# Attention on one Trainium2 core: the softmax division moved from the probabilities to the outputs of a chunk of 512 queries

## The reference

```python
xs = ln_c(x).reshape(N, C, S).transpose(0, 2, 1)        # C = 512, S = 1024
q = xs @ Wq.T + bq;  k = xs @ Wk.T + bk;  v = xs @ Wv.T + bv
# 8 heads of 64
energy = einsum('nhqd,nhkd->nhqk', q, k)
attn = softmax(energy / sqrt(64), axis=3)
out = einsum('nhql,nhld->nhqd', attn, v)
out = out.reshape(N, -1, C) @ Wo.T + bo                 # heads are not moved back beside each other
x = x + out
t = tokens(x);  t = t + ffn(ln_t(t))                    # a three-layer table of nibble arithmetic on a few channels
```

## Time and profile before

| what | value |
|---|---|
| three runs | 2573.52, 2580.71, 2581.93 us |
| median | 2580.71 us |
| the profiled execution | 2580.17 us, its span 2578.4 us |
| PE busy | 2480.2 us, 96% |
| DVE, ACT, POOL busy | 75%, 67%, 35% |
| mean granted clock of PE | 0.991 |
| share of the DMA engines | 27.5% |

### The profile page before, as it was taken

One profiled execution on the slowest core, in us unless ns is written; L12 is line 12 of the kernel. 1 busy time (PEld: TensorE's weight loads), 2 busy tenths in 40 slices (PEclk: granted clock), 3 DMA queues, 4 the chain that ended last, 5 costly groups with the idle time before them and its releaser, 6 DMA issues.

```text
span 2578.4 us, 37154 instructions
## 1 busy us (share of the span) xinstructions
PE 2480.2 (96%) x13216; PEld 2030.9 (79%) x13216; DVE 1928.8 (75%) x3607; ACT 1735.9 (67%) x3083; POOL 893.4 (35%) x804
## 2 busy tenths in 40 slices
PE   7999999999999999999999999999999999999986
PEld 6788878888788787887878878788777887778874
DVE  5777777787777877778677786777867777677766
ACT  4777557775677746777477774777747776477744
POOL 1344414443144432444313433244422444134431
PEclk9999999999999999999999999999999999999997
DMA  7223203341133312224123331232403223033210
GB/s 265 72 70 110 97 28 91 86 131 66 50 82 76 121 66 66 73 72 135 50 68 76 78 130 43 78 85 60 155 17 92 73 70 143 23 93 78 72 64 33
DMA packets 80357, 215.13 MB, mean 83 GB/s; under 512 B 10256, under 2 KB 10416, under 8 KB 74416
## 3 DMA queue, kind: packets, MB, share of 16 engines
q1 hardware_dynamic: 80176, 212.77, 27.5%
HBM read 102.63 MB, written 25.17 MB: 50 GB/s over the span
## 4 chain that ended last, share of the span: by engine, by line
PE 85%; DVE 7%; ACT 4%; issue 1%; POOL 1%; DMA 0%; SPq 0%; ACTq 0%; DVEq 0%
PE pT L462 16%; PE pJ L428 10%; PE pO L477 9%; PE pO L478 9%; PE pS L449 8%; PE pS L450 8%; PE po L612 7%; PE pv L585 7%; PE pv L428 3%; DVE PL L876 2%; DVE nmax L844 1%; PE pt L570 1%; POOL PR L383 1%; ACT PR L692 1%; PE ph L517 1%
## 5 line engine op out<-in xcount | busy, mean ns | idle before, releaser
L383 POOL TENSOR_SCALAR PR<-PR,rinv 128x1024 f32<-128x1024 f32 x512 | 578.5, 1130 | 1240.0 <-DVE rinv L848 1240.0
L726 ACT ACTIVATE PH<-pT 128x512 fp32r<-128x512 f32 x1024 | 557.5, 597 | 361.3 <-PE pT L462 347.7
L876 DVE TENSOR_TENSOR PL<-pT,PH 128x512 fp32r<-128x512 f32 x1024 | 657.4, 684 | 178.1 <-ACT PH L726 176.0
L844 DVE TENSOR_REDUCE nmax<-pS 128x1 f32<-128x1024 f32 x512 | 623.8, 1218 | 150.5 <-PE pS L450 149.5
L692 ACT ACTIVATE PR<-pS,nmax 128x1024 f32<-128x1024 f32 x512 | 574.8, 1123 | 4.7 <-DVE nmax L844 1.5
L462 PEld LDWEIGHTS pT<-ident,PR 128*128 128x128 f32 x4096 | 466.9, 141 | 129.1 <-POOL PR L383 46.0
L462 PE MATMUL pT<-ident,PR 128*128 128x128 f32 x4096 | 545.4, 275 | 22.4 <-DVE PL L876 15.2
L477 PE MATMUL pO<-PH,VS 128*128 128x512 f32 x1024 | 418.1, 408 | 6.3 <-DVE PL L876 6.3
L449 PE MATMUL pS<-KHL,QS 128*128 128x512 f32 x1024 | 411.9, 402 | 5.8 <-DMA KHL<-KHL 3.6
L478 PE MATMUL pO<-PL,VS 128*128 128x512 f32 x1024 | 404.0, 395 | 0.0
L450 PE MATMUL pS<-KHL,QS 128*128 128x512 f32 x1024 | 402.9, 393 | 0.0
(11 more groups left out here) (171 smaller groups left out, 3048.9 us busy)
## 6 DMA issues: line engine op xcount, KB each, us to landing
KHL<-HL SPq DMA_DIRECT2D x192, 256.0 KB, 3.6
X<-in_x SPq DMA_DIRECT2D x64, 512.0 KB, 6.2
WQ<-wqk_split SPq DMA_DIRECT2D x62, 512.0 KB, 4.3
QS<-HL SPq DMA_DIRECT2D x192, 128.0 KB, 3.1
WO<-wo_split SPq DMA_DIRECT2D x16, 1024.0 KB, 6.8
out<-X SPq DMA_DIRECT2D x16, 1024.0 KB, 4.5
KHL<-wv_split SPq DMA_DIRECT2D x14, 1024.0 KB, 8.5
KHL<-KHL SPq DMA_DIRECT2D x16, 512.0 KB, 4.2
```

The source lines that it names most:

```text
L383: pool.tensor_scalar(PR[g % 2][:, :], PR[g % 2][:, :], M["rinv"][:, g:g + 1], 1.0, ALU.mult, ALU.mult)\
L726: act.activation(PH[ck % 2][:, 4 * half:4 * half + 4, (g % 4) * P:(g % 4 + 1) * P], pT[half][:, :].rearrange("p (k n) -> p k n", k=4), ACT ...
L844: dve.tensor_reduce(nmax[:, g:g + 1], pS[g % 2][:, :], AX.X, ALU.max, negate=True).then_inc(S["a_max"], 1)
L876: dve.tensor_tensor(PL[ck % 2][:, ks, qs], pT[half][:, :].rearrange("p (k n) -> p k n", k=4), f32(PH[ck % 2][:, ks, qs]), ALU.subtract).th ...
```

## The change

PR is no longer multiplied: `turn` waits for the exponential alone (a_exp). DVE takes a chunk's four columns of reciprocals in one instruction, 128 a run in place of 512. SP writes them to a row of 512 numbers in memory (`reciprocals_out`, 512 pieces of four bytes) and reads this row back into 64 partitions of RB (`reciprocals_in`), 128 times each. POOL then multiplies the 64×512 outputs in OT by RB and adds b_v (`scale_output`), once per chunk; OB is a plain copy on ACT. The bank pO and OB are now set free by the new semaphore a_osum, which DVE raises after OT = pO + OB; a_o is raised by POOL after both of its operations, and H waits for it. One more small load brings b_v to the lower partitions.

The tables changed with it. The 60 steps between edges are now written into them, in the same order except on POOL, whose row names only the steps that do something. At an edge PE now has T5 to T7 ahead of O0 and O1, V2 and V3 two pieces of B later, P1 ahead of L23 and Y0, and R spread as R0 to R3, R4 R5, R6 R7 between the steps A; ACT has H0 and H1 ahead of the T's and H3 behind N0. The setup pieces W and D3 of START stand at other places, as do F3, H3 and O7's neighbours in LAST.

```diff
-    "a_w0": 48, "a_w1": 48, "a_scores": 64, "a_max": 64, "a_exp": 64, "a_recip": 64, "a_norm": 64, "a_tr": 128,
+    "a_w0": 48, "a_w1": 48, "a_scores": 64, "a_max": 64, "a_exp": 64, "a_recip": 16, "a_row": 256, "a_rows0": 128, "a_rows1": 128, "a_osum": 16, "a_omul": 16, "a_tr": 128,
...
+        rs_s = nc.dram_tensor("rinv_rows", (2 * HEADS, 512), F32, kind="Internal").ap()
...
-    "vector": """H0 H1 E67 T0 H2 T1 T2 T3 T4 T5 O0 T6 T7 O1 H3 O2 N0 O3 O4 O5 O6 O7 B0 U0 U1 B1 B2 U2 U3 V0 U4 U5 U6 U7
+        E57 E58 E59 E60 E61 E62 E63 H0 H1 T0 H2 T1 T2 T3 T4 T5 T6 T7 E67 O0 O1 O2 N0 O3 O4 H3 O5 O6 O7 B0 B1 U0
...
-    "gpsimd": """H0 N0 F0 A0 A1 A2 A3""",
+    "gpsimd": """E7 E8 E11 E12 E15 E16 E19 E20 E23 E24 E27 E28 E31 E32 E35 E36 E39 E40 E43 E44 E47 E48 E51 E52 E56 E60
+        E64 H0 E68 N0 F0""",
...
+    def reciprocals_out(i, ck):
+        wait("a_recip", i, ck + 1)
+        sp.dma_start(dram["rs"][ck].rearrange("(j p) -> p j", p=P), M["rinv"][:, 4 * ck:4 * ck + 4],
+                     allow_slow_non_contiguous=True).then_inc(S["a_row"], 16)
+
+    def reciprocals_in(i, ck):
+        wait("a_row", i, 16 * (ck + 1))
+        if ck >= 2:
+            wait("a_omul", i, ck - 1)
+        elif i > 0:
+            wait("a_omul", i - 1, 2 * HEADS)
+        half = slice(ck % 2 * D, (ck % 2 + 1) * D)
+        sp.dma_start(M["RB"][half, :], dram["rs"][ck].unsqueeze(0).to_broadcast([D, 512])).then_inc(S[f"a_rows{ck % 2}"], 16)
 
...
+        reciprocals_out(i, 0)
...
+                reciprocals_in(i, k)
+                reciprocals_out(i, k + 1)
...
+        reciprocals_in(i, 12)
+        for k in range(2):
+            if i + 1 < N_IMG:
                 wait("a_scores", i, ST * (HEADS - 1 + k))
                 sp.dma_start(f32(WV[k].rearrange("p k n -> p (k n)")), dram["wv"][:, k, :]).then_inc(S["f_wv"], 16)
+            if k == 1:
+                reciprocals_in(i, 13)
+            reciprocals_out(i, 13 + k)
+        reciprocals_in(i, 14)
+        reciprocals_out(i, 15)
         wait("a_pv", i, 2 * HEADS)
         for t in range(CT):
             sp.dma_start(M["X1"][:, t, :], dram["x"][i, :, t, :]).then_inc(S[f"b_x{t}"], 16)
+        reciprocals_in(i, 15)
         if i + 1 < N_IMG:
...
+    def scale_output(img, ck):
+        h, n = divmod(ck, 2)
+        part = slice(n * D, (n + 1) * D)
+        o = M["OT"][part, :, h * P:(h + 1) * P]
+        wait("a_osum", img, ck + 1)
+        wait("a_proj_lo", img, min(ck + 1, PER["a_proj_lo"]))
+        if ck == 2 * HEADS - 1:
+            wait("b_bias", img, 2 * CT)
+        wait(f"a_rows{n}", img, 16 * (h + 1))
+        pool.tensor_tensor(o, o, M["RB"][part, :].rearrange("d (j m) -> d j m", j=CT), ALU.mult).then_inc(S["a_omul"], 1)
+        wait("a_omul", img, ck + 1)
+        pool.tensor_scalar(o, o, M["b_v"][part, h:h + 1], None, ALU.add).then_inc(S["a_o"], 1)
+        wait("a_o", img, ck + 1)
+
     for kind, img, g in order:
...
-        if kind == "A" and 0 <= g < STEPS:
-            wait("a_recip", img, g + 1)
-            pool.tensor_scalar(PR[g % 2][:, :], PR[g % 2][:, :], M["rinv"][:, g:g + 1], 1.0, ALU.mult, ALU.mult)\
-                .then_inc(S["a_norm"], 1)
+        if kind == "A" and 0 <= g < STEPS + 5:
+            if g >= 8 and g % 4 == 0:
+                scale_output(img, g // 4 - 2)
...
-        wait("a_norm", i, g + 1)
+        wait("a_exp", i, g + 1)
...
-                wait("a_o", i, ck)
+                wait("a_osum", i, ck)
...
-                wait("a_o", i, ck - 1)
-            act.activation(OB[ck % 2][:, :], pO[D:P, :], ACT.Identity,
-                           bias=b_v[D:P, ck // 2:ck // 2 + 1]).then_inc(S["a_obot"], 1)
+                wait("a_osum", i, ck - 1)
+            act.activation(OB[ck % 2][:, :], pO[D:P, :], ACT.Copy).then_inc(S["a_obot"], 1)
...
-    def recip(i, g):
-        wait("a_exp", i, g + 1)
-        dve.reciprocal(rinv[:, g:g + 1], rsum[:, g:g + 1]).then_inc(S["a_recip"], 1)
+    def recip(i, ck):
+        wait("a_exp", i, 4 * ck + 4)
+        dve.reciprocal(rinv[:, 4 * ck:4 * ck + 4], rsum[:, 4 * ck:4 * ck + 4]).then_inc(S["a_recip"], 1)
 
     def attend(i, g):
         if g < 0:
             rowmax(i, 0)
             rowmax(i, 1)
-            recip(i, 0)
...
+        if g + 1 < STEPS and g % 4 == 2:
+            recip(i, g // 4)
...
-                              OB[ck % 2][:, :].rearrange("d (j m) -> d j m", j=CT), ALU.add).then_inc(S["a_o"], 1)
```

More of the change, by code:

```diff
@@ L211 @@
-    "gpsimd": """N0 A0 A1 A2 A3""",
+    "vector": """T0 T1 T2 T3 T4 T5 T6 T7 N0 W0 B0 B1 B2 V0 W2 V1 B3 B4 B5 V2 W1 V3 W3 B6 B7 V4 V5 W4 W5 V6 V7 Q0 Q1 Q2
+        A-1 D3 A0 A1 A2 A3""",
+    "gpsimd": """N0""",
 }
 EDGE = {
-    "tensor": """T0 T1 E65 E66 E67 T2 T3 T4 O0 T5 T6 T7 O1 O2 O3 O4 O5 O6 O7 U0 U1 B0 B1 B2 U2 U3 V0 U4 B3 U5 B4 U6 U7 V1
-        V2 V3 B5 B6 B7 V4 V5 V6 F0 F1 V7 F2 F3 L0 Q0 L1 L10 L2 L11 L20 L3 L12 L21 Q1 Q2 L22 L13 P0 L23 P1 Y0 Q3
-        A0 R0 R1 R2 R3 R4 A1 R5 R6 A2 R7 A3""",
@@ L223 @@
-    "gpsimd": """H0 N0 F0 A0 A1 A2 A3""",
+    "tensor": """E4 E5 E6 E7 E8 E9 E10 E11 E12 E13 E14 E15 E16 E17 E18 E19 E20 E21 E22 E23 E24 E25 E26 E27 E28 E29 E30
+        E31 E32 E33 E34 E35 E36 E37 E38 E39 E40 E41 E42 E43 E44 E45 E46 E47 E48 E49 E50 E51 E52 E53 E54 E55 E56
+        E57 E58 E59 E60 E61 E62 E63 T0 T1 E65 E66 E67 T2 T3 T4 T5 T6 T7 O0 O1 O2 O3 O4 O5 O6 O7 U0 U1 B0 B1 B2
+        U2 U3 V0 U4 U5 B3 B4 U6 U7 V1 V2 B5 B6 V3 B7 V4 V5 V6 F0 F1 V7 F2 F3 L0 Q0 L1 L10 L2 L11 L3 L20 Q1 L12
+        L21 Q2 L22 L13 P0 P1 L23 Y0 Q3 A0 R0 R1 R2 R3 A1 R4 R5 A2 R6 R7 A3""",
@@ new lines @@
+    "scalar": """E4 E5 E6 E7 E8 E9 E10 E11 E12 E13 E14 E15 E16 E17 E18 E19 E20 E21 E22 E23 E24 E25 E26 E27 E28 E29 E30
+        E31 E32 E33 E34 E35 E36 E37 E38 E39 E40 E41 E42 E43 E44 E45 E46 E47 E48 E49 E50 E51 E52 E53 E54 E55 E56
+        E57 E58 E59 E60 E61 E62 E63 H0 H1 T0 T1 T2 T3 T4 H2 E67 T5 T6 T7 N0 H3 U0 U1 B0 B1 B2 U2 U3 V0 U4 U5 U6
+        U7 S0 B3 B4 V1 V2 B5 B6 V3 B7 V4 V5 F0 F1 V6 V7 F2 F3 L0 L1 L10 Q0 L2 L11 L20 L3 Q1 L12 L21 Q2 L22 L13
+        L23 A-1 Q3 A0 R0 R1 R2 R3 A1 R4 R5 A2 R6 R7 A3""",
@@ L230 @@
-    "vector": """E67 H0 H1 H2 O0 H3 O1 O2 O3 O4 O5 O6 U0 U1 U2 U3 S10 O7 S15 S11 U4 S12 U5 U6 U7 S13 S20 S25 S21 L0 S22
-        S23 L10 L1 L11 L2 L3 L12 S14 L13 S24""",
-    "gpsimd": """H0 F0 F2""",
+    "tensor": """E4 E5 E6 E7 E8 E9 E10 E11 E12 E13 E14 E15 E16 E17 E18 E19 E20 E21 E22 E23 E24 E25 E26 E27 E28 E29 E30
+        E31 E32 E33 E34 E35 E36 E37 E38 E39 E40 E41 E42 E43 E44 E45 E46 E47 E48 E49 E50 E51 E52 E53 E54 E55 E56
+        E57 E58 E59 E60 E61 E62 E63 E65 E66 E67 O0 O1 O2 O3 O4 O5 O6 U0 U1 U2 U3 O7 U4 U5 U6 U7 F0 F1 L0 L10 F2
+        L1 F3 L20 L11 L2 L21 L3 L12 Y10 L22 L13 R0 R1 R2 L23 R3 Y20 R4 R5 R6 R7""",
@@ new lines @@
+    "scalar": """E4 E5 E6 E7 E8 E9 E10 E11 E12 E13 E14 E15 E16 E17 E18 E19 E20 E21 E22 E23 E24 E25 E26 E27 E28 E29 E30
+        E31 E32 E33 E34 E35 E36 E37 E38 E39 E40 E41 E42 E43 E44 E45 E46 E47 E48 E49 E50 E51 E52 E53 E54 E55 E56
+        E57 E58 E59 E60 E61 E62 E63 E67 H0 H1 H2 H3 U0 U1 U2 U3 S10 U4 U5 U6 U7 S20 F0 F1 L0 L10 L1 F2 L20 F3
+        L11 L2 L3 L21 L12 L22 L13 R0 R1 R2 L23 R3 R4 R5 R6 R7""",
+    "vector": """E4 E5 E6 E7 E8 E9 E10 E11 E12 E13 E14 E15 E16 E17 E18 E19 E20 E21 E22 E23 E24 E25 E26 E27 E28 E29 E30
+        E31 E32 E33 E34 E35 E36 E37 E38 E39 E40 E41 E42 E43 E44 E45 E46 E47 E48 E49 E50 E51 E52 E53 E54 E55 E56
+        E57 E58 E59 E60 E61 E62 E63 E67 H0 H1 H2 O0 O1 O2 O3 O4 H3 O5 O6 U0 U1 U2 U3 S10 O7 S15 S11 U4 U5 U6 S12
+        U7 S13 S20 S25 S21 L0 S22 S23 L10 L1 L11 L2 L3 L12 S14 L13 S24""",
@@ L233 @@
+    "gpsimd": """E7 E8 E11 E12 E15 E16 E19 E20 E23 E24 E27 E28 E31 E32 E35 E36 E39 E40 E43 E44 E47 E48 E51 E52 E56 E60
+        E64 H0 E68 F0 F2""",
 }
@@ L242, in schedule @@
     for i in range(N_IMG):
-        order += [("A", i, g) for g in range(4, 64)] + work(EDGE if i + 1 < N_IMG else LAST, i)
+        order += [("A", i, g) for g in range(4, 4)] + work(EDGE if i + 1 < N_IMG else LAST, i)
     return order
@@ L616, in tensor_program @@
                 wait("b_res", i, 7 if n < ST // 2 else 8)
-                wait(*(("a_proj_out", i, 12), ("a_o", i, 16))[n])
+                wait(*(("a_proj_out", i, 12), ("a_osum", i, 16))[n])
             else:
@@ L674, in scalar_program @@
         "XT", "XH", "OH", "OT", "VS", "QS", "KHL", "PR", "PH", "OB", "X1", "HL", "QK", "WV"))
-    b_qk, b_v, nmax, rsum = (M[k] for k in ("b_qk", "b_v", "nmax", "rsum"))
+    b_qk, nmax, rsum = (M[k] for k in ("b_qk", "nmax", "rsum"))
     pS, pT, pt, pa, ph, pv = ([B[f"{n}{k}"] for k in range(c)] for n, c in (
```

36 lines of the change are left out of this document (14 added, 22 removed).

## The result

| kernel | median of the runs | ratio to the kernel before |
|---|---|---|
| before | 2577.9 us | |
| changed | 2686.8 us (2677.6 to 2687.9) | 1.0414, 95% interval 1.0398 to 1.0429 |

The account below looks back on a forecast made before the run. PE was taken as the bound, busy 2480.2 of 2578.4 us. From 2580.2 us, loop −8, image 0 −2 and edges −3.3 gave 2567 us; the 8-in-10 range was 2550 to 2592.

Parts of the forecast that it names:

- the two small transfers per chunk: SP's row write and read per chunk: 3.6 us landing each, 7.2 us together, hidden in 13.4 us, costing nothing.
- The rival of the late row: At the edge, late rows delay bo's additions and O6: 2591 us at 8.5 us a landing; 15% chance.
- the signs of being wrong: Closing list: loop windows not shortening, PE waiting for OL, landing above 6.7 us, or PE's products at another pace.
- The loop: Steps 4 to 63 of each image: OB earlier 0.5 us, shorter PL waits 0.5 us; 8 us saved in all.
- The waits for PL: PE's three waits per image for PL on DVE, 15.2 us in 24, to shorten to near 12 us.
- the window of 201.00 us: Steps 4 to 63 of an image: PE busy 198.31 us, 2.69 idle, so at most 21.5 us to gain.
- Image 0: Start of the first image: two transposition waits for POOL's product, 1.12 and 0.80 us, go; −2 us.
- The edges: Seven edges between images: 1.05 − 0.32 − 0.45 − 0.75 = −0.47 us each, −3.3 in all.
- The turnover: PE's O0 to O7 at an edge: PE idles 1.8 us before O2, O7 ends 1.05 us later.
- The results' chain: At each edge, DVE's results that R waits for begin 1.15 us earlier without sum wait and reciprocal; taken as −0.75 us.
- The copy of K: At each edge, P1 ahead of L23 and Y0 starts K's copy earlier, removing `scores(0)`'s 0.45 us wait.
- The tail: End of the last image, where H3 has more room: taken with the start as 0, ends ±2 us.

Follow-up runs that it names:

- the kernel with 16-byte pieces: Changed kernel with each row stored in partition order, 128 pieces of 16 bytes instead of 512 of 4, POOL reading RB strided: 2570.1 us, ratio 0.9967.
- the first of the two turnover kernels: Against the kernel with 16-byte pieces: last row read before X1's loads, chunk 15 scaled before bo's additions, turnover tables near their old order: 2563.5 us, ratio 0.9943.

## Why the prediction was wrong

The step that failed is one term: the two small transfers per chunk, priced at a landing of 3.6 us and a cost of nothing. The 3.6 us was that of copies of 256 KB, and the write has 2 KB in 512 pieces of four bytes. The read did land near it (3.9 us). The write took 10.4 and 18.4 us where it was read off the chain, and it costs 122 us, 104 of them through the transfers behind it. With this write taken out the kernel takes 2565.2 us, for a forecast of 2567. That it is so near is in part luck, as the last items below say.

- *The bounds.* The longest landing considered was 12.1 us, the landing of a small load. A load of whole rows says nothing on 512 touching pieces; the range was too narrow because no row resembled the operation and I bounded it all the same. The write was also taken as a latency for whoever waits for it. That is the larger part of the error: 104 us are paid without anyone waiting.
- *The rival of the late row* had 15% and named the right place: X1's loads, the additions of bo, PE at O. Its price of 24.5 us was for 8.5 us a landing; at 12.1 it gave 75, left out of the range, and the edges lost 81. It put PE's wait at O6 for H3; it is at O0's evacuation, since the additions themselves are late (57.4 us of DVE's waits were for them). It had no loop in it: I had written that with a late row only POOL would wait. POOL's queue also holds HL.
- *The Trainium skill*, DMA: Bandwidth & Descriptors, says in "Rules for kernel authors" that a strided last dimension becomes one descriptor per element, and in "Specifications" that pieces under 512 bytes are read, changed and written back. I named it as speaking against the 3.6 us and gave it no price. The runs agree only in part: 512 pieces of four bytes are dear side by side, but 64 bytes apart they land in 3.3 us.
- *The clock.* That PE's own products might follow each other at another pace stood among the signs of being wrong, and no step counted it. It is some 31 of the 122 us.
- *The loop*, −8 us: in the kernel with 16-byte pieces −8.6 (the eight loops sum to 1573.4 us for 1582.0). It is right in size and wrong in its split: OB, priced at 0.5 us an image, gave 0.94. The waits for PL, which were to shorten to 12 us in 24, are 18.2 us in 36. Of the 6.3 us for POOL's product 3.6 lay at step 57 of the images, not at the starts. And the window of 201.00 us is longer than the steps it stood for: within 197.6 us PE is not busy for 2.2, so that the whole of it is 18 us and not 21.5.
- *Image 0*, −2: 10.3 to 8.8 us from step 0 to 4, −1.5, but not by the waits. The time in which PE is not busy there is 2.1 and 2.0 us; its busy time fell from 8.20 to 6.79, since the half-clock stretch that the kernel before has there is absent.
- *The edges*, −0.5 each: +1.3 from the last exponential to the first, −1.5 on average in steps 0 to 4, together −0.2. The turnover was foreseen as +1.05 with PE waiting 1.8 us ahead of O2; it is +1.2 (the last O starts 36.06 us behind the last exponential, for 34.91) with a wait of 1.54. The results' chain gave more than −0.75. The copy of K gave −0.33 (PE's wait is left in one image of eight). The 0.32 us in V3 went, but a later value product waits 0.28 us for XL.
- *The tail*, 0: it was −3.0 us in that profile, 102.7 to 99.7. PE's waits there are the same; its busy time fell from 75.2 to 72.2. In all kernels whose last steps are the same, the tail goes from 98.5 to 102.5 us, with PE busy 70.7 to 75.3 of it and not busy for 27.1 to 27.9. So it is PE's pace, which goes with where the half-clock stretches of the tail fall, and not the change.

## What to carry to other kernels

Before a small transfer is priced as a latency, ask what it does to the queue behind it: time it by issuing it in the old kernel with no one waiting. Lay out a column of numbers from many partitions so that the pieces in memory don't touch, or so that each partition's piece is several numbers; here a changed index order was worth 117 us. A wait of PE can cost more than its length, since the clock may fall in it. And where a row of the profile for an operation is missing, the upper bound must come from a row of the same form or be left wide.

## What was not expected of the hardware

- 128 pieces of 4 bytes side by side land in 8.9 us, 16 bytes apart in 3.2; 512 of them 64, 16 and 8 bytes apart in 3.3, 3.8 and 4.9. Why touching pieces are slow was not settled. The time is not in the pieces' own records (worked out from the packets of the traces, side by side and 64 bytes apart): a packet of 4 bytes takes 10.7 and 10.1 ns in the mean, one of 4096 bytes 327 and 183.
- POOL's addition of one column to 64×512 numbers took 1563 ns (the prediction took 839), where its multiplication and addition of two columns on 128×512 took 906 (L454) and 777 (L460). Not tried further.
- DVE's OL and POOL's scaling take longer when they run side by side, and either may be the one that pays. In the first of the two turnover kernels the pair of OL took 3.72 us; in the kernel with 16-byte pieces it took 2.53 and POOL's product beside it 2.62 in place of 1.55.
